# The last eight neighbour pieces of a two-layer graph kernel: three bf16 passes over fp8 masks replaced by one float32r pass over widened masks

## The chip, the cores and the metric

The kernel runs on one core of one Trainium2 chip. The metric is device time of one launch in microseconds (us), the median of three runs. TensorE (PE) multiplies matrices, VectorE (DVE), ScalarE (ACT) and GpSimd (POOL) work on tiles, SyncE (SP) issues the output transfers.

## The reference

There are 4096 nodes with 64 features, and a symmetric adjacency `adj` with ones on the diagonal. Layer 0 is graph attention over 4096 entities, layer 1 sums neighbours:

```python
h = jnp.maximum(_layernorm(x, axis=-1), 0.0)
x = x + gnn0(h, entity_embs, adj, W, a)      # masked softmax over leaky scores, @ entity_embs, + h, elu
h = jnp.maximum(_layernorm(x, axis=-1), 0.0)
x = x + (matmul((adj == 1).astype(x.dtype), h) + h)
```

The change lies in the last line's product, and only in its last eighth by rows of h times all columns.

## The kernel before, in words

Features lie on partitions (64 for one half of a pair of 512 nodes, 64 for the other), nodes along the free axis; there are NP = 4 pairs p of 2 x 512 nodes. The adjacency arrives as 64 chunks of 128 x 2048 fp8 masks and stays in the 27 slots of `am`. The kernel goes through STEPS_ALL = 128 steps: VectorE makes scores (line 938), ScalarE takes their exponential (line 683), TensorE multiplies by the entities (line 1284) and sums denominators (line 1318). Adding own rows to the masks' diagonals is `own` on GpSimd (line 521).

Layer 1 is cut into 32 **pieces** (p, j), in the order written out in `ORDER`: piece v adds the neighbours in block j (512 nodes, four slices of 128) to pair p. Rows of h are kept in `h3` as three bf16 parts (high, middle, low) whose sum is the f32 value. A slice is 12 matmuls (3 parts x 2 halves s x 2 column strips of 32), by `neighbours` (line 1196), with the 128x512 fp8 mask as the moving operand. Pieces 0 to 16 run among the steps. After step 127 come, in TensorE's order: the last denominators (line 1305), slices 0 to 5 of the rest, `spread` (line 1146), slices 6 to 12, `rows_turned` (line 1172), slices 13 to 27, and, once `lasts` on VectorE has written the third part of the last pair's rows (line 909, `h_ready`), slices 28 to 59. The last 32 of them are pieces 24 to 31, two for each pair, because they need blocks j = 6 and 7, which are the last pair's own rows. Piece 19 is the last of pair 0 before the final eight and consists of slices 8 to 11.

Beside them runs the finish of pair 3, which each engine does in its own program order: `sums_out` (ACT, lines 592 to 594), `inverses` (DVE, 860 to 863), `spread` (PE), `weighted` (DVE, 872 and 873), `negatives` (ACT, 606 and 608), `rows_on` (DVE, 878 and 879), `rows_turned` (PE), `rows_normed` (DVE, 888 to 896, with `deviations` on POOL, 512 and 513), then `highs`, `rests`, `middles`, `lasts`. At the end VectorE takes each pair's sums with one instruction (line 990), and SyncE sends it out (line 424):

```python
for p in range(NP):
    dve.wait_ge(piece_done, 26 + 2 * p)
    v.scalar_tensor_tensor(out=yp[:, p, 0:HALF], in0=gather(24 + 2 * p), scalar=-1.0, in1=xs[:, p],
                           op0=ALU.add, op1=ALU.add).then_inc(out_ready, 1)
```

Of the kernel before, what the change touches and what calls it, by code (L numbers as in the profile page):

```python
# [62 lines left out]
def graph_layers(nc, adj_t, xt, ent, w_t, a_cols, eye, out, N, M, D):  # L63
# [110 lines left out]
    with ctx:  # L174
        def sb(name, shape, dt):
            return ctx.enter_context(nc.sbuf_tensor(name, shape, dt))
# [92 lines left out]
        def diagonal(v):  # L269
            p, j = ORDER[v]  # L270
            slot, at = chunk_at(chunk0[j % 2] + j) if p == 0 else chunk_at(chunks_of(p, j)[0])
            step = HALF + P if p == 0 else 2 * HALF + P
            at += slot * UNIT + (j % 2 * HALF if p else 0)
            return am_flat[:, at:at + SUB * step].rearrange("p (i k) -> p i k", k=step)[:, :, 0:P]

        def part(k):
            return h0[:, (0, 1, 0)[k]]
# [131 lines left out]
        def own_at(v):  # L409
            return PIECE_AT[v] - 3  # L410

        block = ctx.enter_context(nc.Block())

        @block.sync
        def _(sp):
            sp.dma_start(enta[:], ent).then_inc(ld_ent, 16)
            sp.dma_start(mats[:], eye).then_inc(ld_eye, 16)
            sp.dma_start(xs[:, 0:1], xt[:, 0:1]).then_inc(ld_x, 16)

            sp.wait_ge(landed[landed_of(chunk0[1] - 1)[0]], landed_of(chunk0[1] - 1)[1])  # L420
            sp.dma_start(xs[:, 1:NP], xt[:, 1:NP]).then_inc(ld_late, 16)
            for p in range(NP):
                sp.wait_ge(out_ready, p + 1)
                sp.dma_start(out[p], yp[:, p, 0:HALF]).then_inc(out_done, 16)
            sp.wait_ge(out_done, 16 * NP)

        @block.gpsimd
        def _(pool):
# [109 lines left out]
                    if w < PIECES and n == own_at(w):  # L538
                        own(w)
            for w in OWN:  # L540
                if PIECES <= w < OPENS[-1] + 2:
                    own(w)
            deviations(NP - 1)
            for w in OWN[6:]:
                own(w)

        @block.scalar
        def _(act):
# [127 lines left out]
            for n in range(STEPS_ALL):  # L676
                b, jt = block_at(n)
                act.wait_ge(y_made, n + 1)
                m = 2 // HALVES[b]
                for r in range(m):  # L680
                    y = yp[:, n % YS, r * HALF:r * HALF + width(b)]
                    at = jt * m + r
                    e = sc.activation(y, y, ACT.Exp, bias=tbias[:, at:at + 1], scale=delta[:, 0:1])  # L683
                e.then_inc(exp_done, 1)
                for p, f in NORM.items():
                    if n == f["sq"]:
                        squares_first(p)
# [24 lines left out]
                if b + 1 < NB:  # L712
                    if b >= 1 and jt == SROWS[b] + 1:
                        s_rows(b)
                    for h in range(first[b + 1], first[b + 2]):
                        if n == VOUT[b + 1]:
                            v_rows(b + 1, h)
            sums_out(NB - 1)
            negatives(NP - 1)
            highs(NP - 1)  # L720
            middles(NP - 1)

        @block.vector
        def _(dve):
# [199 lines left out]
            for n in range(STEPS_ALL):  # L924
# [41 lines left out]
                if b + 1 < NB:  # L966
                    if n == READ[b + 1]:
                        read_sums(b + 1)
                    for h in range(first[b + 1], first[b + 2]):
                        if n == LARGEST[b + 1]:  # L970
                            largest(b + 1, h)
                    if n == LARGEST[b + 1]:
                        shifts(b + 1)
                    if n + 1 == start_of[b + 1]:
                        put_codes(b + 1, 0)
            for r in range(2):
# [3 lines left out]
                v.tensor_tensor(yp[:, SUM_IN[r] % YS], yp[:, n % YS], yp[:, (n + 1) % YS], ALU.add).then_inc(y_summed, 1)  # L980
            inverses(NP - 1)
            weighted(NP - 1)
            rows_on(NP - 1)
            rows_normed()
            rests(NP - 1)
            lasts(NP - 1)
            for p in range(NP):
                dve.wait_ge(piece_done, 26 + 2 * p)

                v.scalar_tensor_tensor(out=yp[:, p, 0:HALF], in0=gather(24 + 2 * p), scalar=-1.0, in1=xs[:, p],  # L990
                                       op0=ALU.add, op1=ALU.add).then_inc(out_ready, 1)

        @block.tensor
        def _(pe):
# [180 lines left out]
            def neighbours(v, i):  # L1175
# [16 lines left out]
                for k in range(3):  # L1192
                    for s in range(2):
                        for d in range(0, D, 32):
                            at = s * D + d
                            mm = t.matmul(gather(v)[at:at + 32, :], h3[:, jt, k * D + d:k * D + d + 32],  # L1196
                                          masks(v, i, s),
                                          start=(v in OPENS and i == 0 and k == 0),
                                          stop=((v in VISITS or j == NH - 1) and i == SUB - 1 and k == 2),
                                          tile_position=(0, at))  # L1200
                if i == SUB - 1:
                    mm.then_inc(piece_done, 1)
# [181 lines left out]
```

## Time and profile before

| | |
|---|---|
| median of 3 runs | 354.31 us (353.14 to 354.66) |
| the profiled execution's own time | 352.26 us |
| its span, first to last instruction | 350.5 us |
| around the span | 1.76 us |
| granted TensorE clock, mean | 1.00 |
| PE / DVE / ACT / POOL busy | 92% / 79% / 58% / 22% of the span |

The profiled execution lies 2.05 us under the median. Times inside the span count from its start. An engine executes its instructions in program order, so a wait holds all that is written behind it on the same engine.

### The profile page before, as it was taken

Reading aid. Unit: us, or ns where it says so; the run is one execution under the profiler, and the core shown is the slowest. Engines: PE = TensorE matmul, PEld = TensorE weight load, DVE = VectorE, ACT = ScalarE, POOL = GpSimd, SP = SyncE. Lnnn points to the kernel's source line nnn. Section 1 sums busy time; section 2 is a strip of 40 time slices with the busy share of each in tenths; the row PEclk is TensorE's granted clock in tenths of the full one; section 3 lists DMA queues with packets and bytes.
Section 4 is the critical chain, followed back from the end, with each engine's and each line's share of the span. In section 5 each row is a group of like instructions: output and inputs, shape, how many; then the busy total and the mean of one; then the engine's idle time right before and its main releaser. Section 6 shows DMA issues by size and latency. Waiting matters only on the chain.

```text
span 350.5 us, 8710 instructions
## 1 busy us (share of the span) xinstructions
PE 322.8 (92%) x3857; PEld 129.0 (37%) x3857; DVE 277.7 (79%) x344; ACT 203.6 (58%) x263; POOL 77.7 (22%) x118
## 2 busy tenths in 40 slices
PE   0279799999999989999999999999999999999996
PEld 0244344333332232342333433443334333345553
DVE  0682799999999999999998799899984999455201
ACT  1010388679959789657865977385749667330000
POOL 4663258821212121013002400000008000004000
PEclk9999999999999999999999999999999999999999
DMA  8999999999999999358003950000000000000011
GB/s 201 113 101 155 127 108 107 108 108 107 108 108 108 107 108 108 37 47 77 2 2 34 90 60 2 2 3 2 2 0 4 0 2 2 2 2 2 2 64 60
DMA packets 10564, 20.85 MB, mean 59 GB/s; under 512 B 1248, under 2 KB 1312, under 8 KB 10400
## 3 DMA queue, kind: packets, MB, share of 16 engines
q0 software_dynamic: 9216, 16.78, 48.4%
q1 hardware_dynamic: 1152, 3.49, 2.8%
q8 instruction: 30, 0.49, 0.6%
q10 hardware_dynamic: 160, 0.03, 0.0%
q14 instruction: 6, 0.05, 0.0%
HBM read 69.58 MB, written 1.05 MB: 202 GB/s over the span
## 4 chain that ended last, share of the span: by engine, by line
PE 50%; DVE 24%; issue 3%; ACT 1%; POOL 1%; DVEq 0%; POOLq 0%
PE pb L1284 18%; DVE yp L938 14%; PE pb L1196 11%; PE pb L1318 8%; PE pa L1196 8%; DVE coded L827 2%; PE pa L1076 1%; PE pa L1161 1%; PE pa L1153 1%; DVE um L806 1%; PE pa L1029 1%; PE pa L1146 1%; DVE rows L851 1%; POOL rstd L513 0%; PE pa L1089 0%
## 5 line engine op out<-in xcount | busy, mean ns | idle before, releaser
L683 ACT ACTIVATE yp<-yp,tbias,delta 128x1024 f32<-128x1024 f32 (+1 forms) x160 | 162.2, 1067 | 36.6 <-DVE yp L938 36.4
L938 DVE SCALAR_TENSOR_TENSOR yp<-s8b,t8neg,coded 128x1024 f32<-128x1024 f32 (+1 forms) x160 | 161.7, 1065 | 1.9 <-PE pb L1318 0.8
L1284 PE MATMUL pb<-yp,enta 128*32 128x512 f32 x1024 | 130.2, 594 | 2.8 <-ACT yp L683 2.6
L1318 PE MATMUL pb<-yp,onesf 128*32 128x512 f32 x496 | 64.6, 593 | 0.0
L1196 PE MATMUL pb<-am,h 128*32 128x512 fp8e4 x960 | 61.1, 379 | 0.0
L449 POOL DMA_DIRECT2D am<-adj_t x64 | 34.7, 556 | 104.8 <-PE pb L1196 53.1
L1284 PEld LDWEIGHTS pb<-yp,enta 128*32 128x32 f32 x1024 | 30.3, 110 | 57.8 <-issue 32.4
L1196 PEld LDWEIGHTS pb<-am,h 128*32 128x32 bf16 x960 | 28.0, 97 | 44.1 <-issue 30.0
L827 DVE TENSOR_TENSOR coded<-am,vx 128x2048 uint16<-128x2048 uint16 (+1 forms) x33 | 41.4, 1255 | 2.4 <-ACT vx L578 1.1
L1196 PE MATMUL pa<-am,h 128*32 128x512 fp8e4 x576 | 33.8, 379 | 0.2 <-DVE h L909 0.2
L512 POOL TENSOR_SCALAR rstd<-rstd 128x8 f32<-128x8 f32 x4 | 2.2, 544 | 126.3 <-ACT rstd L619 78.8
L1318 PEld LDWEIGHTS pb<-yp,onesf 128*32 128x32 f32 x496 | 15.7, 110 | 23.2 <-issue 17.7
L1196 PEld LDWEIGHTS pa<-am,h 128*32 128x32 bf16 x576 | 16.3, 97 | 20.5 <-issue 9.0
L1076 PE MATMUL pa<-am,gtab 128*32 128x512 fp8e4 x256 | 21.2, 411 | 0.9 <-DVE gtab L770 0.9
L1076 PEld LDWEIGHTS pa<-am,gtab 128*32 128x32 bf16 x256 | 6.7, 100 | 17.3 <-issue 15.3
L799 DVE TENSOR_SCALAR gmax<-pa,wk 128x1024 f32<-128x1024 int32 (+1 forms) x5 | 5.3, 1064 | 6.2 <-PE pa L1076 6.2
L513 POOL TENSOR_TENSOR rstd<-rstd,mhalf 128x8 f32<-128x8 f32 x4 | 9.5, 2379 | 0.3
L998 PE MATMUL pa<-num 64*128 64x64 f32 x2 | 0.7, 444 | 9.6 <-DVE num L740 9.6
L521 POOL TENSOR_TENSOR am<-am,eyeb 128x512 fp8e4<-128x512 fp8e4 x8 | 9.5, 1210 | 0.0
L990 DVE SCALAR_TENSOR_TENSOR yp<-pa,xs 128x512 f32<-128x512 f32 x2 | 1.4, 692 | 10.0 <-PE pa L1196 10.0
L606 ACT ACTIVATE tm<-ta 128x512 f32<-128x512 f32 x4 | 2.5, 631 | 11.2 <-DVE ta L873 11.2
L479 POOL TENSOR_TENSOR rstd<-rstd,mhalf 128x8 f32<-128x8 f32 x4 | 8.8, 2193 | 0.3
(184 smaller groups left out, 227.3 us busy)
## 6 DMA issues: line engine op xcount, KB each, us to landing
am<-adj_t POOLq DMA_DIRECT2D x64, 256.0 KB, 22.2
enta<-ent SPq DMA_DIRECT2D x1, 1040.0 KB, 5.1
out<-yp SPq DMA_DIRECT2D x4, 256.0 KB, 2.0
xs<-xt SPq DMA_DIRECT2D x1, 768.0 KB, 9.3
mats<-eye SPq DMA_DIRECT2D x1, 320.0 KB, 7.8
xs<-xt SPq DMA_DIRECT2D x1, 256.0 KB, 11.0
num<-w_t ACTq DMA_DIRECT2D x1, 32.0 KB, 5.3
a_sb<-a_cols ACTq DMA_DIRECT2D x1, 0.5 KB, 8.0
```

Source lines behind the costliest of these rows:

```text
L449: pool.dma_start(am[:, slot, at:at + CHUNK], adj_t[q]).then_inc(landed[landed_of(q)[0]], 16)
L479: g.tensor_tensor(rstd0[:, p], rstd0[:, p], mhalf[:], ALU.pow).then_inc(sd_ready, 1)
L513: g.tensor_tensor(rstd[:], rstd[:], mhalf[:], ALU.pow).then_inc(rstd_ready, 1)
L521: g.tensor_tensor(e, e, eyeb[:].unsqueeze(1).to_broadcast([P, SUB, P]), ALU.add, saturate=False).then_inc(own_ready, 1)
L683: e = sc.activation(y, y, ACT.Exp, bias=tbias[:, at:at + 1], scale=delta[:, 0:1])
L799: link(v.tensor_scalar(gmax[:, 0:W], sums, wk[:], None, ALU.min))
L827: return v.tensor_tensor(coded[:].bitcast(U16).rearrange("p (t i) -> p t i", t=t)[:, lo:hi], am[:, slot_of[U]].bitcast(U16).rearrange("p ( ...
L938: y = v.scalar_tensor_tensor(out=yp[:, n % YS, r * HALF:r * HALF + W], in0=s8b[:, pair(b) % 2, cols(b)], scalar=t8neg[:, at:at + 1], in1=c ...
L1076: mm = t.matmul(pa[g * KC:(g + 1) * KC, first[b] % 2 + i], gtab[:, jt], am[:, slot, at:at + HALF], start=(k == 0), stop=(k == NQ - 1), til ...
L1196: mm = t.matmul(gather(v)[at:at + 32, :], h3[:, jt, k * D + d:k * D + d + 32], masks(v, i, s), start=(v in OPENS and i == 0 and k == 0), s ...
L1284: t.matmul(acc2(b)[k:k + 32, :], enta[:, at, d:d + 32], yp[:, n % YS, s * HALF:(s + 1) * HALF], start=(jt == 0), stop=final, tile_position ...
L1318: mm = t.matmul(dens[at:at + 32, :], onesf[:, 0:32], yp[:, (m + r) % YS, s * HALF:(s + 1) * HALF], start=(opens and m + batch == n + 1), s ...
```

## The change

The last eight pieces (v = 24 to 31, slices counted k = 0 to 31) no longer go through `neighbours`. The last pair's rows are stored in `hr` as two float32r parts side by side, high in columns 0 to 63 and rest in columns 64 to 127, and one matmul of 128 rows x 128 columns x 512 gives both products for one half: 2 matmuls a slice, 64 in all, each with its mask as a float32r tile. The masks are widened from fp8 by copies of 128 x 1024 elements (two of 128 x 512 for pair 0). They go into 12 free slots of `am` and the 7 buffers `yp`, so 19 (ROOM) fit; slice k from 19 on takes the place of slice k - 19 and waits for `slice_done`. Each pair's two halves sit in two PSUM banks, in which the two parts still have to be added, and pair 2 reuses pair 0's banks.

Three steps of the old finish (`highs`, `rests`/`middles`/`lasts` of the last pair) become one ScalarE copy and one VectorE subtraction (`hr_ready`). GpSimd's last `own` calls for pieces 30 and 31 come ahead of `deviations`.

```diff
+        FREE = sorted((k for k in range(SLOTS) if k not in late_slots), key=slot_done)
+        ROOM = len(FREE) + YS
+        def wide_masks(k):
+            r = k % ROOM
+            return amr[:, FREE[r]] if r < len(FREE) else ypr[:, r - len(FREE)]
+        EARLY = dict(d0=(0,), a0=(1, 3, 5, 7, 9), p0=(2, 6, 10), d1=(4, 8, 11), a1=(12, 13), d2=(14,),
+                     a2=(15, 16, 17, 18))
+        LATE = range(ROOM, 32)
+        LATE_BY = {k: "adap"[(k - ROOM) % 4] for k in LATE}
+        def last_bank(p, s):
+            return (pb[:, 2 * s], pa[:, 2 + s])[p % 2]
+        def wait_wide(eng, k):
+            v, i = slice_of(k)
+            if k >= ROOM:
+                eng.wait_ge(slice_done, k - ROOM + 1)
+            elif k < len(FREE):
+                eng.wait_ge(piece_done, slot_done(FREE[k]) + 1)
+                eng.wait_ge(coded_ready, NU)
+            else:
+                eng.wait_ge(pv_done, STEPS_ALL)
+            if v in OWN:
+                eng.wait_ge(own_ready, OWN.index(v) + 1)
 ...gpsimd, behind the loop over the steps
             for w in OWN:
-                if PIECES <= w < OPENS[-1] + 2:
+                if w >= PIECES:
                     own(w)
+            for k in EARLY["p0"]:
+                widen(k)
             deviations(NP - 1)
-            for w in OWN[6:]:
-                own(w)
+            for k in late("p"):
+                widen(k)
 ...scalar
+            for k in EARLY["a0"]:
+                widen(k)
             sums_out(NB - 1)
+            for k in EARLY["a1"]:
+                widen(k)
             negatives(NP - 1)
-            highs(NP - 1)
-            middles(NP - 1)
+            for k in EARLY["a2"]:
+                widen(k)
+            act.wait_ge(hh_ready, NP)
+            sc.copy(hr[:, :, 0:D], natural(NP - 1)[0]).then_inc(high_ready, 1)
+            for k in late("a"):
+                widen(k)
 ...vector, in rows_normed, ahead of the wait for rstd_ready
+                sums_so_far(3)
+                sums_so_far(1)
 ...vector, behind the steps
+            def sums_so_far(p):
+                last = max(w for w in range(LAST) if ORDER[w][0] == p)
+                dve.wait_ge(piece_done, last + 1)
+                v.scalar_tensor_tensor(out=xs[:, p], in0=gather(last), scalar=-1.0, in1=xs[:, p],
+                                       op0=ALU.add, op1=ALU.add).then_inc(so_far, 1)
+            def last_sums(p):
+                for s in range(2):
+                    if p == NP - 1 and s == 0:
+                        dve.wait_ge(half_done, 1)
+                    else:
+                        dve.wait_ge(slice_done, 8 * (p + 1))
+                    own, other = slice(s * D, (s + 1) * D), slice((1 - s) * D, (2 - s) * D)
+                    link(v.tensor_tensor(xs[own, p], last_bank(p, s)[other], xs[own, p], ALU.add))
+                    o = v.tensor_tensor(s8b[own, p // 2, ...], last_bank(p, s)[own], xs[own, p], ALU.add)
+                    if s:
+                        o.then_inc(out_ready, 1)
+            widen 0
             (the two sums of line 980)
+            widen 4, 8, 11
             inverses(NP - 1)
+            widen 14
             weighted(NP - 1)
+            sums_so_far(0)
             rows_on(NP - 1)
             rows_normed()
-            rests(NP - 1)
-            lasts(NP - 1)
-            (one instruction of line 990 for each pair)
+            dve.wait_ge(high_ready, 1)
+            v.tensor_tensor(hr[:, :, D:2 * D], natural(NP - 1)[0], hr[:, :, 0:D].bitcast(F32),
+                            ALU.subtract).then_inc(hr_ready, 1)
+            sums_so_far(2)
+            widen 20, 24
+            last_sums(0)
+            widen 28
+            last_sums(1), last_sums(2), last_sums(3)
 ...tensor
-            pieces(range(13, (len(ORDER) - PIECES) * SUB))
+            pieces(range(13, (LAST - PIECES) * SUB))
+            pe.wait_ge(hr_ready, 1)
+            for p in range(NP):
+                if p >= 2:
+                    pe.wait_ge(out_ready, p - 1)
+                both_halves = [(k, s) for k in range(8 * p, 8 * p + 8) for s in range(2)]
+                if p == NP - 1:
+                    both_halves.sort(key=lambda ks: ks[1])
+                for k, s in both_halves:
+                    pe.wait_ge(wide[e], BY[e].index(k) + 1)
+                    mm = t.matmul(last_bank(p, s), hr[:, k % 8], wide_masks(k)[:, s * HALF:(s + 1) * HALF],
+                                  start=(k % 8 == 0), stop=(k % 8 == 7))
```

## Rows read from the trace of the kernel before

**Rows 1.** The page's busy tenths in 40 slices of the span.

```profile
PE   0279799999999989999999999999999999999996
DVE  0682799999999999999998799899984999455201
PEclk9999999999999999999999999999999999999999
```

**Rows 2.** The chain that ended last: start, length in us, what.

```profile
301.94 3.43 PE pb L1284 x32
...
306.24 3.89 PE pa L1196 x72
...
311.11 4.65 PE pa L1196 x84
...
326.41 10.54 PE pa L1196 x192
347.36 0.69 DVE yp L990
```

**Rows 3.** Busy time by engine in the last stretch of TensorE.

```profile
326.40:347.40 21.00, 20.90 (x384) 11.44 (x384) 2.11 (x4) 0.00 (x0) 0.00 (x0) 1.00 0.11 40
```

**Rows 4.** Timeline from the last masks' coding to the third part of h.

```profile
292.52 1.23 DVE L827 TENSOR_TENSOR coded<-am,vx 128x2048 uint16<-128x2048 uint16 x1
...
298.79 1.28 DVE L938 SCALAR_TENSOR_TENSOR yp<-s8b,t8neg,coded 128x1024 f32<-128x1024 f32 x1 [0.85 <-PE pb L1318]
300.11 1.25 ACT L683 ACTIVATE yp<-yp,tbias,delta 128x1024 f32<-128x1024 f32 x1 [0.89 <-DVE yp L938]
...
306.30 0.58 ACT L592 COPY rows<-pb 64x512 f32<-64x512 f32 x1 [4.95 <-PE pb L1305]
...
310.05 0.15 PEld L1146 LDWEIGHTS pa<-rows,mats 64*32 64x32 f32 x8 [0.42 <-DVE rows L863]
...
313.95 0.69 DVE L878 SCALAR_TENSOR_TENSOR ta<-ta,tm 128x512 f32<-128x512 f32 x1 [1.36 <-ACT tm L608]
314.68 0.69 DVE L879 TENSOR_TENSOR xs<-ta,xs 128x512 f32<-128x512 f32 x1
...
315.69 0.66 PE L1172 MATMUL pa<-mats,xs 128*128 128x128 f32 x4
...
316.28 4.72 PE L1196 MATMUL pa<-am,h 128*32 128x512 fp8e4 x84
...
321.74 2.60 POOL L521 TENSOR_TENSOR am<-am,eyeb 128x512 fp8e4<-128x512 fp8e4 x2
321.86 1.52 DVE L896 TENSOR_TENSOR rs<-tm,rstd 128x512 f32<-128x512 f32 x1 [1.88 <-POOL rstd L513]
...
324.06 0.82 DVE L904 TENSOR_TENSOR rs<-rs,h 128x512 f32<-128x512 f32 x1 [0.68 <-ACT h L636]
```

**Rows 5.** Timeline of 128-column f32 weights: loads and matmuls.

```profile
35.64 1.62 PEld L1207 LDWEIGHTS pb<-enta,onesf 128*128 128x128 f32 x8
35.75 1.92 PE L1207 MATMUL pb<-enta,onesf 128*128 128x260 f32 x8
```

**Rows 6.** Groups of instructions by form: busy, mean ns.

```profile
L683 ACT ACTIVATE yp<-yp,tbias,delta 128x1024 f32<-128x1024 f32 x96 | 115.5, 1240 | 28.7 <-DVE yp L938 28.5
...
L636 ACT CAST h<-rs 128x512 bf16<-128x512 f32 x4 | 2.5, 618 | 9.6 <-DVE rs L896 9.5
...
L851 DVE TENSOR_SCALAR rows<-vx 3x1024 bf16<-3x1024 uint8 x3 | 2.0, 674 | 0.0
```

**Rows 7.** Timeline where GpSimd and VectorE work at once, two places.

```profile
47.46 5.37 DVE L938 SCALAR_TENSOR_TENSOR yp<-s8b,t8neg,coded 128x512 f32<-128x512 f32 x8
50.58 2.32 POOL L478 TENSOR_SCALAR rstd<-rstd 128x8 f32<-128x8 f32 x1 [1.86 <-ACT rstd L657]
...
158.88 3.29 DVE L827 TENSOR_TENSOR coded<-am,vx 128x2048 uint16<-128x2048 uint16 x1
158.90 2.18 POOL L521 TENSOR_TENSOR am<-am,eyeb 128x512 fp8e4<-128x512 fp8e4 x2
```

More of the change, by code:

```diff
@@ L8 @@
 BF16 = mybir.dt.bfloat16
+F32R = mybir.dt.float32r
 FP8 = mybir.dt.float8e4
@@ L182, in sem @@
             return ctx.enter_context(nc.semaphore(name))
-        am = sb("am", [P, SLOTS, UNIT], FP8)
-        coded = sb("coded", [P, UNIT], U8)
-        yp = sb("yp", [P, YS, 2 * HALF], F32)
+        with ExitStack() as loop_only:
+            am = loop_only.enter_context(nc.sbuf_tensor("am", [P, SLOTS, UNIT], FP8))
+            coded = loop_only.enter_context(nc.sbuf_tensor("coded", [P, UNIT], U8))
+            yp = loop_only.enter_context(nc.sbuf_tensor("yp", [P, YS, 2 * HALF], F32))
+        amr = sb("amr", [P, SLOTS, 2 * HALF], F32R)
+        hr = sb("hr", [P, 2 * SUB, 2 * D], F32R)
+        ypr = sb("ypr", [P, YS, 2 * HALF], F32R)
         s8b = sb("s8b", [P, 2, 2 * HALF], F32)
@@ L274, in diagonal, with slot_done, slice_of, narrow_masks @@
             return am_flat[:, at:at + SUB * step].rearrange("p (i k) -> p i k", k=step)[:, :, 0:P]
+        LAST = 24
+        late_slots = {chunk_at(q)[0] for v in range(PIECES, len(ORDER)) for q in chunks_of(*ORDER[v])}
+        def slot_done(k):
+            return max(last_piece(U) for U in range(NU) if slot_of[U] == k)
+        FREE = sorted((k for k in range(SLOTS) if k not in late_slots), key=slot_done)
+        ROOM = len(FREE) + YS
+        def slice_of(k):
+            return LAST + 2 * (k // 8) + k % 8 // SUB, k % SUB
+        def wide_masks(k):
+            r = k % ROOM
+            return amr[:, FREE[r]] if r < len(FREE) else ypr[:, r - len(FREE)]
+        def narrow_masks(k):
+            v, i = slice_of(k)
+            w = wide_masks(k)
+            if ORDER[v][0] == 0:
+                return [(w[:, s * HALF:(s + 1) * HALF], masks(v, i, s)) for s in range(2)]
+            slot, at = chunk_at(chunks_of(*ORDER[v])[i // 2])
+            at += i % 2 * 2 * HALF
+            return [(w, am[:, slot, at:at + 2 * HALF])]
+        EARLY = dict(d0=(0,), a0=(1, 3, 5, 7, 9), p0=(2, 6, 10), d1=(4, 8, 11), a1=(12, 13), d2=(14,),
+                     a2=(15, 16, 17, 18))
+        LATE = range(ROOM, 32)
+        LATE_BY = {k: "adap"[(k - ROOM) % 4] for k in LATE}
+        def late(e):
+            return [k for k in LATE if LATE_BY[k] == e]
+        BY = {e: [k for n in sorted(EARLY) if n[0] == e
+                  for k in EARLY[n]] + late(e) for e in "adp"}
+        def last_bank(p, s):
+            return (pb[:, 2 * s], pa[:, 2 + s])[p % 2]
         def part(k):
@@ L395, in graph_layers @@
         out_ready = sem("out_ready")
+        wide = {e: sem(f"wide_{e}") for e in "adp"}
+        slice_done = sem("slice_done")
+        half_done = sem("half_done")
+        so_far = sem("so_far")
+        high_ready = sem("high_ready")
+        hr_ready = sem("hr_ready")
         def unit_of(j):
@@ L410, in own_at @@
             return PIECE_AT[v] - 3
+        def wait_wide(eng, k):
+            v, i = slice_of(k)
+            if k >= ROOM:
[7 more added lines that the diff above has]
+                eng.wait_ge(own_ready, OWN.index(v) + 1)
         block = ctx.enter_context(nc.Block())
@@ L423, in _ @@
                 sp.wait_ge(out_ready, p + 1)
-                sp.dma_start(out[p], yp[:, p, 0:HALF]).then_inc(out_done, 16)
+                sp.dma_start(out[p], s8b[:, p // 2, p % 2 * HALF:(p % 2 + 1) * HALF]).then_inc(out_done, 16)
             sp.wait_ge(out_done, 16 * NP)
@@ L540, in _, with widen @@
             for w in OWN:
-                if PIECES <= w < OPENS[-1] + 2:
+                if w >= PIECES:
                     own(w)
+            def widen(k):
+                wait_wide(pool, k)
+                for dst, src in narrow_masks(k):
+                    w = g.tensor_copy(dst, src)
+                w.then_inc(wide["p"], 1)
+            for k in EARLY["p0"]:
+                widen(k)
             deviations(NP - 1)
-            for w in OWN[6:]:
-                own(w)
+            for k in late("p"):
+                widen(k)
         @block.scalar
@@ L717, in _, with widen @@
                             v_rows(b + 1, h)
+            def widen(k):
+                wait_wide(act, k)
+                for dst, src in narrow_masks(k):
+                    w = sc.copy(dst, src)
+                w.then_inc(wide["a"], 1)
+            for k in EARLY["a0"]:
+                widen(k)
             sums_out(NB - 1)
+            for k in EARLY["a1"]:
+                widen(k)
             negatives(NP - 1)
-            highs(NP - 1)
-            middles(NP - 1)
+            for k in EARLY["a2"]:
[4 more added lines that the diff above has]
+                widen(k)
         @block.vector
@@ L975, in _, with widen @@
                         put_codes(b + 1, 0)
+            def widen(k):
+                wait_wide(dve, k)
+                for dst, src in narrow_masks(k):
+                    w = v.tensor_copy(dst, src)
+                w.then_inc(wide["d"], 1)
+            def sums_so_far(p):
+                last = max(w for w in range(LAST) if ORDER[w][0] == p)
+                dve.wait_ge(piece_done, last + 1)
+                if p == NP - 1:
+                    dve.wait_ge(hn_ps, NP)
+                v.scalar_tensor_tensor(out=xs[:, p], in0=gather(last), scalar=-1.0, in1=xs[:, p],
[8 more added lines that the diff above has]
+                    link(v.tensor_tensor(xs[own, p], last_bank(p, s)[other], xs[own, p], ALU.add))
+                    o = v.tensor_tensor(s8b[own, p // 2, p % 2 * HALF:(p % 2 + 1) * HALF], last_bank(p, s)[own],
+                                        xs[own, p], ALU.add)
+                    if s:
+                        o.then_inc(out_ready, 1)
+            for k in EARLY["d0"]:
+                widen(k)
             for r in range(2):
@@ L980, in _ @@
                 v.tensor_tensor(yp[:, SUM_IN[r] % YS], yp[:, n % YS], yp[:, (n + 1) % YS], ALU.add).then_inc(y_summed, 1)
+            for k in EARLY["d1"]:
+                widen(k)
             inverses(NP - 1)
+            for k in EARLY["d2"]:
+                widen(k)
             weighted(NP - 1)
+            sums_so_far(0)
             rows_on(NP - 1)
             rows_normed()
-            rests(NP - 1)
-            lasts(NP - 1)
[L987 to L991, printed above, removed]
+            dve.wait_ge(high_ready, 1)
+            v.tensor_tensor(hr[:, :, D:2 * D], natural(NP - 1)[0], hr[:, :, 0:D].bitcast(F32),
+                            ALU.subtract).then_inc(hr_ready, 1)
+            sums_so_far(2)
+            dve.wait_ge(so_far, NP)
+            d = late("d")
+            for k in d[0:2]:
+                widen(k)
+            last_sums(0)
+            for k in d[2:]:
+                widen(k)
+            for p in range(1, NP):
+                last_sums(p)
         @block.tensor
@@ L1198, in neighbours @@
                                           start=(v in OPENS and i == 0 and k == 0),
-                                          stop=((v in VISITS or j == NH - 1) and i == SUB - 1 and k == 2),
+                                          stop=((v in VISITS or j == NH - 3) and i == SUB - 1 and k == 2),
                                           tile_position=(0, at))
```

6 lines of the change are left out of this document (added).

## The prediction

> **What bounds the kernel now.** I read the page's busy tenths first, then the chain that ended last, then the busy time of the last stretch, then the timeline from 292 us on. The page shows TensorE at nine tenths in nearly every slice from 125 us to the end, at full granted clock, and VectorE falling away in the last sixth [rows 1]. The chain says the same of the end: from 301.9 us it consists of TensorE's matmuls but for a passage through VectorE, and after the last matmul only one instruction of VectorE and the output transfer follow [rows 2]. The last eight pieces are 384 matmuls in 20.90 us with no idle time, and the other compute engines have 2.11 us of work between them there [rows 3]. So TensorE bounds the stretch that is changed, and nothing else is near it.
>
> The stretch ahead of it (306 to 326 us) is TensorE's too, but barely. `spread` loads its weights at 310.05, released by the inverse, and in the chain slices 0 to 5 run until 310.13 (306.24 + 3.89). `rows_on` ends at 315.37 (314.68 + 0.69), the transposes start at 315.69, which is when slices 6 to 12 run out (311.11 + 4.65). Two meeting points, with slack of 0.1 and 0.3 us [rows 2, 4]. Whatever makes the finish of pair 3 later there is paid in full.
>
> **TensorE's last stretch.** Removed: 32 slices of 12 matmuls. 72 of them take 3.89 us, so a slice takes 0.648 us, and four strips of 512 columns side by side take 0.216 us, one column per cycle of 2.4 GHz [rows 2]. Added: 64 float32r matmuls with 512 columns each. No row has one. Its price is bounded from below by the one-pass products' 0.216 us, and from above by one record of an f32 product: an f32 product is two records here, four strips take 3.43 us / 32 x 4 = 0.429 us a record, so a whole f32 product costs 0.858 us, four times a one-pass one [rows 2]. If f32 is four partial products, float32r, given here two parts cut by hand, is one of them: I take 0.216. A second price is the weight load: each matmul loads 128 x 128 f32 weights. The eight records of 260 columns with such weights take 1.92 us, 0.24 us or less each, and their loads lie beside them [rows 5]. A load thus fits behind 0.22 us of matmul, and I charge nothing; exposed it would be charged to each of the 64. So a slice takes 0.43 us instead of 0.648, and the 32 take 13.8 us.
>
> The rows give 0.216 by an argument and not by a measurement. The Trainium skill, FP8 and Floating Point Precision, section TensorE Precision Notes, says that true FP32 is four passes and that reduced-precision FP32 reads 4 bytes and truncates to FP22; the trace agrees with the four. By it the stretch is the same 13.8 us.
>
> **Its tail is VectorE's.** The old end is one 0.69 us instruction for a pair. The new one is four for a pair (`last_sums`), each on 64 partitions x 512 with a PSUM input; at 0.69 us (line 878, same columns) plus 0.03 between them, 0.72 [rows 4]. Let T be the start of the float32r matmuls. Pair 0 ends at T + 3.46, its sums at T + 6.6, before pair 2 wants the banks (T + 6.9). Widening 28 (0.67) and pair 1's sums run to T + 10.2, before pair 3's matmuls at T + 10.37. Pairs 2 and 3 then give eight instructions in a row from T + 10.37 + 0.23 (release as before: 326.41 + 384 x 0.054 = 347.13, then 347.36 [rows 2, 3]): end at T + 10.6 + 8 x 0.72 = T + 16.36. TensorE itself is done at T + 13.8. So VectorE becomes the end's bound: 2.56 us lie behind TensorE's end instead of 0.92, and 1.6 of the 7.1 us that TensorE saves are lost.
>
> **Widening.** ScalarE: a cast of 512 takes 0.618, a 1024 instruction 1.24 with a bias [rows 6]; I take 0.61 and 1.04 (0.618 + 512 x 0.83 ns; bounds 0.9 and 1.24). VectorE: one source in SBUF, 1024 elements, 0.674, and 0.41 for half of it [rows 6]; the upper bound is 1.28, the two-source price [rows 4]. GpSimd: no row of this size; from ScalarE's 0.61 to 1.09 for 512 (half of 2.18, two sources) [rows 6, 7]; I take 0.8, 1.6 for 1024. Late ones: ScalarE has seven, each freed by slice k - 19; 31 is freed at T + 5.6 and wanted at T + 13. At 1.04 each it is done by T + 9. VectorE has three, GpSimd three (freed at T + 1.7, 3.4, 5.2, wanted 7.7 us later). TensorE waits for none. GpSimd's 22 may overlap VectorE's 24; I charge 0.25 for that.
>
> **What the early ones do to the finish.** This is where the change costs.
> 1. ScalarE does slices 1, 3, 5, 7, 9 ahead of `sums_out`. Its last exponential ends at 301.36, `sums_out` starts at 306.30: 4.94 us of room [rows 4]. The work is 8 x 0.61 + 1.04 = 5.9 us, with starts overlapping a little or gaps of 0.03: `sums_out` starts 0.75 to 1.25 late, I take 1.0. The inverse is late by it, and so is `spread`, which has no slack: TensorE stands for 1.0 us.
> 2. GpSimd now does own 31 (released at 293.75, when the last masks are coded) and slices 2, 6, 10 there, 1.1 + 4 x 0.8 + 1.6 = 5.9 us beside VectorE's last steps [rows 4]. The two get in each other's way: a coding instruction (1.23 elsewhere [rows 4]) took 3.29 beside GpSimd's 2.18, so it waited for nearly all of it; elsewhere a 0.2 us job of GpSimd took 2.32 and VectorE's eight ran at 0.67 as always [rows 7]. Who loses differs. VectorE had 0.85 us to spare before its last step [rows 4]. If it loses 3.5 us (four instructions each behind one of GpSimd), the last exponential is 2.6 late; if it wins, nothing. I take 0.6, added to point 1, since ScalarE has no room left.
> 3. `sums_so_far(0)` stands ahead of `rows_on` and waits for piece 19, that is for slice 11, six slices after `spread`. Without shifts slice 11 ends at 311.11 + 3.89 = 315.0, VectorE starts at 315.2; then 0.72, 0.72, 0.69: 317.33 instead of 315.37. TensorE wants it at 315.69 and gets it at 317.4: stands for 1.7 us. It is relative to `spread`, so it adds to points 1 and 2.
>
> At no cost: slice 0 on VectorE (the last step ends at 300.07 or 0.6 later, then 0.82 and the two sums of line 980, 1.28 at most each: 304.1, while TensorE wants them at 301.94 + 3.43 = 305.4 [rows 2, 4]); 4, 8, 11 (2.2 us from there to 306.3, and the denominators are copied out by 306.30 + 2 x 0.6 = 307.5, 1.6 later with the shifts); 14 (in the wait for `spread`); 12, 13 on ScalarE (2.1 us; `sums_out` ends after three copies at 308.1, `negatives` are two instructions of 0.65 that end at 313.92: 4.5 us between them [rows 4]); 15 to 18 (4.2 us, while VectorE norms for 8 us, 315.37 to 323.38); `sums_so_far(3)` and `(1)` in the wait for the reciprocal root (1.9 us [rows 4]), though (1) waits for slice 19 and ends about when the root does. The rows: cast 0.62, subtraction 0.83 [rows 4, 6] end 9.5 us after `rows_on`, and 0.7 earlier without own 30 and 31 beside line 896. TensorE comes 10.7 us after `rows_on` (transposes 0.6, 15 slices 9.7, 0.3), so the two dropped steps win nothing: there the end was TensorE's slices already.
>
> **Sum.** T without shifts is 316.28 + 15 x 0.648 = 326.0. With 1.0 + 0.6 + 1.7 it is 329.3. The end of VectorE's last instruction is 329.3 + 16.36 + 0.25 = 345.9, against 348.05: 2.15 us less. The profiled execution goes from 352.26 to 350.1, and 2.05 us lie between it and the median: 354.31 - 2.15 = 352.2. A measurement of this kernel can tell 0.5% (1.8 us) from no change, so faster is under 352.5 and slower over 356.1; the forecast is just over the line.
>
> A page speaks against the change. The Trainium skill, Advanced Engine Details and Errata, section VectorE Performance Modes (Mode Summary), notes that VectorE's second SBUF port is GpSimd's too and that GpSimd and two-port instructions of VectorE block each other. The case above in which coding took 3.29 us agrees, with two sources as well. What it would do here is rival B.
>
> **Rivals.**
> A. The front costs little: ScalarE's copies fit the 4.94 us and only point 3 stays (T = 327.7), or that goes too. End 344.3 to 342.6, so 350.6 to 348.9. For it: starts may overlap; against: 5.9 us of work in 4.9. Chance 0.13.
> B. GpSimd's 5.9 us come on top of VectorE's last steps: point 2 is 2.6 instead of 0.6, 354.2. If all of it does (5.9 - 0.85 = 5.1), 356.7. Chance 0.17.
> C. The other side: the float32r matmul isn't 0.216. T + 64c + 0.23 + 1.44 (half 0 of pair 3 is summed meanwhile) equals the old 348.05 at c = 0.267 us; above it the kernel is slower. At 0.429, two cycles per column as in an f32 record, the end is 329.3 + 27.5 + 1.7 = 358.5: 364.7. If the load stays exposed (1.62 us / 8 = 0.2 at most, 0.11 if half overlaps), c is 0.33 to 0.42, 358.3 to 364. For it: no row shows four-byte columns faster than two cycles. Chance 0.11.
> D. Late widening or the banks hold TensorE: 1 to 2 us, 353.7. Chance 0.07.
> The forecast, 350.7 to 353.7, has 0.52. Of it, 0.35 are under 352.5. With A: faster 0.48. B's first half, D and the rest: same 0.39. C and the end of B: slower 0.13. The range, 349.3 to 356.0, leaves out C and the ends of A and B.
>
> **What would show it.** PE L1196 loses 384 matmuls and 64 of 128x512 f32 come in their place, 0.216 us apart; at 0.43 C holds. ScalarE's copy of line 592 starts about 1.6 us later than 306.30 and directly behind a widening; if behind a wait for TensorE, A holds. VectorE waits for TensorE ahead of `sums_so_far(0)`, and TensorE stands about 1.7 us ahead of the transposes. VectorE's last eight instructions are back to back. VectorE instructions of lines 938 and 980 over 1.3 us beside GpSimd's copies speak for B. Wrong at once: a lower granted clock after the two stands of TensorE; before it there is none [rows 1].

## The result, and the profile after

The median went from 353.48 us (8 runs, 352.15 to 355.18) to 351.15 us (8 runs, 350.55 to 352.32): a ratio of 0.9938, with a 95% interval of 0.9916 to 0.9961, 2.2 us less by the ratio (1.4 to 3.0). The forecast was 0.994. The profiled execution took 351.37 us, with a span of 349.6. The part that is changed is larger than the text ahead of the prediction says: pieces 24 to 31 are 8 of 32 and take blocks 6 and 7 of 8, so it is the last quarter of the product by rows of h, not the last eighth.

The page of the changed kernel, busy tenths in 40 slices of 8.74 us:

```profile
PE   0379799999999989999999999999999999988994
DVE  0781897999999999999998789899985999976586
ACT  1010477688959689666865978285839585875160
PEclk9999989999999999999999999999999999999999
```

VectorE, which was down to 0 to 2 tenths at the end [rows 1], now has 5 to 8. TensorE has an 8 at slices 36 and 37, where it stood. The chain that ended last, from the last masks' coding on (start, length, what; parts under 0.1 us left out where marked):

```profile
295.82 3.60 DVE yp L1031 x3
...
300.88 1.64 DVE yp L1031
...
303.69 5.19 ACT amr L798 x9
...
308.90 0.58 ACT rows L668
...
312.63 1.06 PE pa L1281 x8
313.70 4.03 PE pa L1331 x72
317.73 0.02 issue
317.75 0.69 DVE xs L1082
...
319.82 0.66 PE pa L1307 x4
320.48 4.65 PE pa L1331 x84
325.12 5.18 PE pb L1331 x96
330.30 3.86 PE pb L1480 x16
334.16 3.63 PE pa L1480 x16
337.79 3.64 PE pb L1480 x16
341.43 0.02 issue
341.45 0.70 DVE xs L1092
...
346.46 0.69 DVE s8b L1093
```

This is the new course of the end. VectorE's steps lead to ScalarE's nine copies (line 798), those to `sums_out` (668) and, through the inverse, to `spread` (1281); six slices (72 matmuls) lead to `sums_so_far(0)` (1082) and only that to the transposes (1307). From 330.3 it is the float32r matmuls (1480), and after pair 2's it leaves TensorE and goes through eight instructions of VectorE to the end; the last 16 matmuls aren't on it.

The runs differ early, so I count from an anchor: the start of the last 32 f32 matmuls of the steps, 301.76 in the old trace, 302.36 in the new one. Times behind it, in us:

| | before | after |
|---|---|---|
| last denominators (L1305 / L1440) | 3.43 | 4.40 |
| `sums_out` (L592 / L668) | 4.54 | 6.54 |
| `spread` (L1146 / L1281) | 8.29 | 10.27 |
| transposes (L1172 / L1307) | 13.93 | 17.46 |
| first matmul of the last eight pieces (L1196 / L1480) | 24.65 | 27.88 |
| end of VectorE's last instruction | 46.29 | 44.79 |

From the anchor on the changed kernel is 1.50 us shorter; 0.60 of that does not show between the two profiled executions, because the second reached its anchor later.

The timeline of the changed kernel shows the three places where TensorE stood (0.78 us ahead of the last denominators, 0.92 ahead of `spread`, 1.48 ahead of the transposes):

```profile
288.24 5.72 DVE L1031 SCALAR_TENSOR_TENSOR yp<-s8b,t8neg,coded 128x1024 f32<-128x1024 f32 x4
288.35 2.14 POOL L588 TENSOR_TENSOR am<-am,eyeb 128x512 fp8e4<-128x512 fp8e4 x1 [15.49 <-DVE coded L918]
...
295.36 1.42 POOL L588 TENSOR_TENSOR am<-am,eyeb 128x512 fp8e4<-128x512 fp8e4 x1 [4.88 <-DVE coded L918]
...
295.74 6.77 DVE L1031 SCALAR_TENSOR_TENSOR yp<-s8b,t8neg,coded 128x1024 f32<-128x1024 f32 x4
...
296.73 7.43 POOL L614 CAST amr<-am 128x512 fp32r<-128x512 fp8e4 x5
...
302.55 1.24 ACT L759 ACTIVATE yp<-yp,tbias,delta 128x1024 f32<-128x1024 f32 x1 [0.31 <-DVE yp L1031]
...
306.76 1.06 PE L1440 MATMUL pb<-yp,onesf 128*32 128x512 f32 x8 [0.78 <-DVE yp L1104]
...
308.90 0.58 ACT L668 COPY rows<-pb 64x512 f32<-64x512 f32 x1
...
317.75 0.69 DVE L1082 SCALAR_TENSOR_TENSOR xs<-pa,xs 128x512 f32<-128x512 f32 x1 [2.57 <-PE pa L1331]
...
319.82 0.66 PE L1307 MATMUL pa<-mats,xs 128*128 128x128 f32 x4 [1.48 <-DVE xs L970]
```

Four of VectorE's step instructions took 6.77 us beside GpSimd's copies, where one took 1.28 [rows 4], and the last exponential ended 1.43 us behind the anchor instead of 0.40 ahead of it (301.36). `sums_out` has no wait in brackets: it follows ScalarE's own copies. VectorE waited 2.57 us for slice 11, and TensorE 1.48 us for VectorE.

In the old kernel there was one stand in this stretch too, which the rows ahead of the prediction leave out. Slices 13 to 27 ran out at 326.0 us, `lasts` ended at 326.26, and TensorE began the last eight pieces at 326.41, released by it:

```profile
325.57 0.69 DVE L909 TENSOR_TENSOR h<-rs,h 128x512 bf16<-128x512 f32 x1 [0.69 <-ACT h L641]
...
326.41 10.54 PE L1196 MATMUL pa<-am,h 128*32 128x512 fp8e4 x192 [0.24 <-DVE h L909]
```

The float32r matmuls by line (duration, first and last start), 26 of the 64:

```profile
L1480 PEld LDWEIGHTS pb<-amr,hr x26: 186/188/189, 330.2 to 340.8; 128*128 128x128 f32 x26
L1480 PE MATMUL pb<-amr,hr x26: 389/389/501, 330.2 to 341.0; 128*128 128x512 f32 x26
```

The 64 run from 330.24 to 345.04; less one duration of 0.39 that is 14.41 / 63 = 0.229 us apart, not 0.429 and not quite 0.216. The mean holds one longer gap of 0.34 us behind the first; the median gap is 0.227, the figure in the expectations below.

### The profile page after: what moved, and what is told of

The parts are those of the page before. It is cut to its first block, busy times and chain, and to the rows that moved or that the text cites. A ratio compares the mean times of both kernels' runs of the same rounds, so it can differ in the third digit from the quotient of the medians.

```text
span 349.6 us, 8138 instructions
## 1 busy us (share of the span) xinstructions
PE 319.3 (91%) x3537; PEld 130.6 (37%) x3537; DVE 296.4 (85%) x369; ACT 220.8 (63%) x284; POOL 91.3 (26%) x126
## 4 chain that ended last, share of the span: by engine, by line
PE 36%; DVE 33%; ACT 5%; issue 4%; DVEq 0%; ACTq 0%
DVE yp L1031 21%; PE pb L1419 12%; PE pb L1331 9%; PE pb L1453 6%; DVE coded L918 3%; PE pa L1331 2%; PE pb L1480 2%; ACT yp L759 2%; ACT amr L798 1%; PE pa L1480 1%; PE pa L1288 1%; PE pa L1211 1%; DVE xs L1092 1%; DVE s8b L1093 1%; DVE um L897 1%
## 5 line engine op out<-in xcount | busy, mean ns | idle before, releaser
L1031 DVE SCALAR_TENSOR_TENSOR yp<-s8b,t8neg,coded 128x1024 f32<-128x1024 f32 (+1 forms) x160 | 164.4, 1082 | 1.1
L1331 PE MATMUL pb<-am,h 128*32 128x512 fp8e4 x768 | 50.6, 379 | 0.0
L1331 PEld LDWEIGHTS pb<-am,h 128*32 128x32 bf16 x768 | 22.2, 97 | 39.5 <-issue 29.9
L579 POOL TENSOR_SCALAR rstd<-rstd 128x8 f32<-128x8 f32 x4 | 1.1, 274 | 99.6 <-ACT rstd L695 79.9
L1331 PE MATMUL pa<-am,h 128*32 128x512 fp8e4 x384 | 23.3, 379 | 0.0
L1331 PEld LDWEIGHTS pa<-am,h 128*32 128x32 bf16 x384 | 10.6, 97 | 15.4 <-issue 8.3
L798 ACT CAST amr<-am 128x512 fp32r<-128x512 fp8e4 (+1 forms) x15 | 11.0, 814 | 3.7 <-PE pb L1480 3.7
L546 POOL TENSOR_TENSOR rstd<-rstd,mhalf 128x8 f32<-128x8 f32 x4 | 12.7, 3170 | 0.3
L614 POOL CAST amr<-am 128x512 fp32r<-128x512 fp8e4 (+1 forms) x8 | 10.6, 1345 | 8.1 <-PE pb L1480 7.3
L580 POOL TENSOR_TENSOR rstd<-rstd,mhalf 128x8 f32<-128x8 f32 x4 | 9.4, 2362 | 0.3
L654 ACT CAST vx<-pa 128x512 uint8<-128x512 f32 x8 | 4.3, 574 | 7.0 <-PE pa L1242 7.0
```

The lines of the kernel that those rows point to most:

```text
L546: g.tensor_tensor(rstd0[:, p], rstd0[:, p], mhalf[:], ALU.pow).then_inc(sd_ready, 1)
L614: w = g.tensor_copy(dst, src)
L798: w = sc.copy(dst, src)
L1031: y = v.scalar_tensor_tensor(out=yp[:, n % YS, r * HALF:r * HALF + W], in0=s8b[:, pair(b) % 2, cols(b)], scalar=t8neg[:, at:at + 1], in1=c ...
```

## The experiments

All are edits of the changed kernel. Where no number of runs is given, the time is of one run. The times alone scatter by over 1 us, so what is compared first is the time behind the anchor, in us:

| | sums_out | spread | transposes | first of the last eight pieces | end |
|---|---|---|---|---|---|
| before | 4.54 | 8.29 | 13.93 | 24.65 | 46.29 |
| after | 6.54 | 10.27 | 17.46 | 27.88 | 44.79 |
| e1 | 6.52 | 10.25 | 15.89 | 26.31 | 43.22 |
| e2 | 4.71 | 8.44 | 15.63 | 26.04 | 42.96 |
| e3 | 5.52 | 9.27 | 16.46 | 26.87 | 43.79 |
| e4 | 4.54 | 8.29 | 13.93 | 24.34 | 41.27 |
| c1 | 5.20 | 8.93 | 16.12 | 26.53 | 43.44 |
| g1 | 5.51 | 9.24 | 16.43 | 26.84 | 43.75 |
| n1 | 6.54 | 10.27 | 17.46 | 27.87 | 44.13 |
| n2 | 6.54 | 10.27 | 17.46 | 27.87 | 44.86 |
| n3 | 4.54 | 8.29 | 13.93 | 24.35 | 40.61 |
| e5 | 4.54 | 8.29 | 13.93 | 24.34 | 40.59 |
| n4 | 4.54 | 8.29 | 13.93 | 24.35 | 39.78 |

**e1**, `sums_so_far(0)` behind `rows_on`:

```diff
-            sums_so_far(0)
             rows_on(NP - 1)
+            sums_so_far(0)
```

> sums_so_far(0) moved behind rows_on, where VectorE waits for the transposes anyway. Ledger theory (each stand of TensorE ahead of its meeting point is a cost of its own): in the changed kernel the transposes start 7.19 us after spread (312.63 to 319.82), here 5.6 us, so the float32r matmuls start 1.55 us earlier relative to spread, and the end is 1.5 us earlier. Rival (the chain of rows was as late anyway, a loss moves to the next meeting point): the transposes are earlier, but TensorE then stands ahead of the float32r matmuls, and the end is less than 0.5 us earlier.

Measured: 348.64 us. From `spread` to the transposes 5.64 us instead of 7.19, and the end 1.57 us earlier, both counted behind the anchor: the whole stand comes back. The ledger theory holds. The instruction itself costs nothing there:

```profile
316.04 0.69 DVE L970 TENSOR_TENSOR xs<-ta,xs 128x512 f32<-128x512 f32 x1
316.65 0.68 DVE L1082 SCALAR_TENSOR_TENSOR xs<-pa,xs 128x512 f32<-128x512 f32 x1
317.05 0.42 PEld L1307 LDWEIGHTS pa<-mats,xs 128*128 128x128 f32 x4 [0.42 <-DVE xs L970]
```

**e2**, GpSimd idle early:

```diff
-  p0=(2, 6, 10), ... a2=(15, 16, 17, 18)
+  p0=(), ... a2=(15, 16, 17, 18, 2, 6, 10)
-                if w >= PIECES:
+                if PIECES <= w < LAST:
                     own(w)
             deviations(NP - 1)
+            (own(w) for w >= LAST)
```

> GpSimd makes no early copies (slices 2, 6, 10 go to ScalarE behind 15 to 18) and adds the own rows of pieces 30 and 31 behind the reciprocal root, as before the change. Ledger theory (GpSimd beside VectorE's last steps made those late): the last steps of line 1031's kind take 1.28 us each again instead of up to 2, the last exponential ends about 2 us earlier, TensorE's stand of 0.8 us ahead of the last denominators goes, and the stand ahead of spread becomes under 1 us instead of 0.93 behind the 0.78: end 1.5 to 2.0 us earlier. Rival (ScalarE's five copies alone make sums_out late): less than 0.5 us.

Measured: 350.45 us, and 1.83 us less behind the anchor. The steps are what they were before:

```profile
295.75 3.67 DVE L1034 SCALAR_TENSOR_TENSOR yp<-s8b,t8neg,coded 128x1024 f32<-128x1024 f32 x3
...
301.58 1.25 ACT L762 ACTIVATE yp<-yp,tbias,delta 128x1024 f32<-128x1024 f32 x1 [0.89 <-DVE yp L1034]
...
302.73 5.19 ACT L801 CAST amr<-am 128x512 fp32r<-128x512 fp8e4 x9
...
307.94 0.58 ACT L671 COPY rows<-pb 64x512 f32<-64x512 f32 x1
```

ScalarE's five slices are still ahead of `sums_out`, take 5.19 us, and make it 0.17 late (4.71 against 4.54). So they alone cost 0.17, and GpSimd's work on top of them 1.83.

**e3**, ScalarE's copies spread out: `a0=(1, 3), a1=(5, 7, 9), a2=(12, 13, 15, 16, 17, 18)`.

> ScalarE makes only slices 1 and 3 ahead of sums_out, 5, 7, 9 behind it, 12 and 13 behind negatives. Ledger theory: sums_out waits for TensorE and no longer for ScalarE; spread starts 0.9 to 1.2 us earlier relative to the last denominators, the 0.8 us stand ahead of those stays, end 1.0 us earlier. Rival (VectorE's copies 4, 8, 11 end just then and hold the inverse): the inverse waits for VectorE instead, under 0.4 us.

Measured: 349.83 us, 1.00 us less behind the anchor; `sums_out` now has a wait for TensorE in its bracket:

```profile
307.32 0.58 ACT L668 COPY rows<-pb 64x512 f32<-64x512 f32 x1 [2.04 <-PE pb L1440]
```

As expected. Its 1.0 and e2's 1.83 are not two costs: GpSimd's work makes ScalarE start late, and ScalarE's copies pass the lateness on. Either cure takes away the part that goes through ScalarE; the rest of the 2.00 (0.98 in e3) is the late last denominators.

**e4**, the three together.

> The three together. Ledger theory: all stands between 302 and 330 us go (0.8 + 0.9 + 1.5, and the slack), the float32r matmuls start where slices 13 to 27 would end without any, near 326.2 us plus what the run is late before, the tail stays 16.9 us: 3.5 to 4 us under the changed kernel, about 347.4 us where it is 351.2, 6 us under the old one. Rival (gains don't add, the rows of h become the bound of the float32r start): 2 us under the changed kernel at most.

Measured: 349.51 us (6 runs, 347.06 to 350.25), ratio to the old kernel 0.9874 (0.9837 to 0.9911). `sums_out`, `spread` and the transposes are the old kernel's to 0.01 us. The float32r matmuls start 3.54 us earlier than in the changed kernel, when slices 13 to 27 are done, and 0.31 us earlier than the old kernel's last eight pieces. 3.52 us less behind the anchor, as the ledger has it; the rival falls. The medians show less than that (1.6 us), because e4's runs had the lower granted clock of the last section more often. At the same mean clock the difference is there: at 0.998 to 0.999 the changed kernel took 350.55 to 350.94 us and e4 347.06, at 0.994 they took 352.22 to 352.32 and 348.61 to 349.21.

**c1**, own rows of 30 and 31 late, GpSimd's copies early, and **g1**, the reverse (p0 empty, own rows early as in the change).

> The changed kernel, but GpSimd adds the own rows of pieces 30 and 31 behind the reciprocal root again; its five copies stay where they are. It tells which of GpSimd's jobs make VectorE's last steps late: two of 512 elements with two sources (3.6 us busy), or five copies (7.4 us busy). Theory (copies): sums_out starts within 0.6 us of the changed kernel's 6.54 us behind the anchor (the start of the last 32 f32 matmuls of the steps). Rival (own rows): it starts at 5 us or below.

> GpSimd adds the own rows of pieces 30 and 31 early as in the changed kernel, but makes no early copies (they go to ScalarE behind 15 to 18). With own rows late and copies early sums_out started 5.2 us behind the anchor, with neither 4.71, with both 6.54. Theory (the two jobs use up one and the same slack of VectorE, so each alone costs little and only both together cost 1.8 us): here 4.7 to 5.2. Rival (the two-source additions are the dear ones): 5.9 to 6.1.

Measured: 349.27 and 349.42 us. `sums_out` is at 5.20 with the copies alone and 5.51 with the own rows alone, 4.71 with neither, 6.54 with both: 0.49, 0.80 and 1.83. Both statements of c1 were off (copies are not the dear part, own rows are not all of it), and g1 lies between its two. Together the jobs cost more than the sum of both (1.29). The durations of VectorE's steps show why:

```profile
L1034 DVE SCALAR_TENSOR_TENSOR yp<-s8b,t8neg,coded x9: 1279/1285/1630, 284.9 to 298.8; 128x1024 f32<-128x1024 f32 x9
L1031 DVE SCALAR_TENSOR_TENSOR yp<-s8b,t8neg,coded x9: 1271/1275/2129, 284.8 to 299.3; 128x1024 f32<-128x1024 f32 x9
```

In c1 (first line) four steps took 1.63 us beside the copies, in g1 (second line) two took 2.13 beside the additions, and all others 1.28. So VectorE lost 4 x 0.35 = 1.4 us in c1, 2 x 0.85 = 1.7 in g1, and 2 x 0.85 + 3 x 0.35 = 2.75 in the changed kernel, which had both. Its slack of 0.85 us [rows 4] is there only once: 0.55, 0.85 and 1.9 are left, and the last exponential ended 0.48, 0.78 and 1.82 us later than in e2.

**n1**, pair 2's fold left out:

```diff
+                    if p != 2:
                         link(v.tensor_tensor(xs[own, p], last_bank(p, s)[other], xs[own, p], ALU.add))
```

> Leaves out the two adds of the second part to pair 2's sums (2 of VectorE's last 8 instructions, so pair 2's output lacks that part). Theory (VectorE sets the end, TensorE is 0.7 us behind it): from the first float32r matmul to the end 16.3 us instead of 16.9, after which pair 3's second half waits for TensorE. Rival (TensorE or the output sets it): 16.9 us.

Measured: 350.03 us; first matmul to end 16.26 instead of 16.91. Two instructions of 0.69 less gave 0.65, since then VectorE waits for TensorE:

```profile
343.20 0.68 DVE L1094 TENSOR_TENSOR s8b<-pa,xs 64x512 f32<-64x512 f32 x1
343.86 0.39 PE L1481 MATMUL pa<-ypr,hr 128*128 128x512 f32 x1
344.29 0.68 DVE L1093 TENSOR_TENSOR xs<-pa,xs 64x512 f32<-64x512 f32 x1 [0.40 <-PE pa L1481]
```

**n2**, `hr[:, k % 8, 0:D]` as weights, written to the first 64 partitions of each bank; the other 64 are not written, so the output is not the product.

> The float32r matmuls take the high part alone as weights (64 columns instead of 128; the rest part is left out of the result). It tells why they come 0.227 us apart and not 0.216. Theory (the load of 128 columns of four bytes, 0.188 us beside each matmul, costs the difference): 0.216 apart, TensorE's last matmul 0.6 to 0.7 us earlier behind the first. Rival (four-byte columns cost it themselves): 0.227 again.

Measured: 353.6 us; TensorE is busy for 14.94 us instead of 14.80. The load fell from 188 to 134 ns and the pace did not get better (median gap 0.230 us, not 0.227): my theory of the load falls. The rival's 0.227 was not met exactly either.

**n3**, two bf16 parts, masks as they are:

```diff
-                    mm = t.matmul(last_bank(p, s), hr[:, k % 8], wide_masks(k)[:, s * HALF:(s + 1) * HALF],
+                    mm = t.matmul(last_bank(p, s), hr[:, k % 8, 0:2 * D], masks(v, i, s),
```

> No float32r and no widening: the rows in two bf16 parts (high and middle; the low part is left out) side by side as weights of 128 columns, the masks in fp8 as they are, sums_so_far(0) behind rows_on, GpSimd's own rows of 30 and 31 late. It shows what is left of the plan without any widening, and the pace of a two-byte 128-column pass. Theory: the meeting points are those of the old kernel (3.4, 8.3, 13.9 us behind the anchor), 0.216 us a matmul, 16.4 us from the first of them to the end, 40.8 us from anchor to end. Rival (the pace of 0.227 belongs to 128-column weights of any type): 41.3.

Measured: 348.54 us. 13.99 us from the first of the 64 matmuls to TensorE's end, (13.99 - 0.38) / 63 = 0.216 apart with the same 128 columns of weights. So 0.013 us a matmul, 0.8 us in 64, belongs to the float32r operands and not to the width of the weights. And the meeting points are e4's: in e4 widening costs nothing beside that pace. It also shows where TensorE's gain comes from: the old slice of 0.648 us is three times 0.216, one for each bf16 part, and two parts take two, in bf16 as in float32r.

**e5**, e4 with ScalarE's help for pair 2, and **n4**, n3 with the same:

```diff
+            act.wait_ge(slice_done, 24)
+            for s in range(2):
+                f = sc.copy(num[own], last_bank(2, s)[other])
+            f.then_inc(folded, 1)
 ...vector, for pair 2
+                for s in range(2):
+                    o = v.tensor_tensor(xs[own, 2], last_bank(2, s)[own], xs[own, 2], ALU.add)
+                link(o)
+                dve.wait_ge(folded, 1)
+                v.tensor_tensor(s8b[:, 1, 0:HALF], num[:], xs[:, 2], ALU.add).then_inc(out_ready, 1)
```

> e4 and ScalarE copies pair 2's two other halves out of PSUM side by side, so VectorE needs three instructions for pair 2 instead of four. Theory (VectorE's eight instructions in a row set the end, 0.65 us to be had before TensorE does): from the first float32r matmul to the end 16.25 us instead of 16.93, anchor to end 40.6, the time 0.6 us under e4 and 13 us per thousand under the old kernel. Rival (ScalarE's copies come too late, or the two read PSUM in each other's way): 16.9 or more.

> n3 (two bf16 parts side by side, the low part left out, no widening, no stands) with the same help of ScalarE. Theory: 15.6 us from the first matmul of the last eight pieces to the end, anchor to end 39.9 us, 6.4 us under the old kernel and 0.7 under e5. Rival: the pace or the tail is not what sets it, 40.6.

Measured: e5 346.43 us (5 runs, 346.07 to 348.02), ratio 0.9795 (0.9772 to 0.9818); n4 345.54 us (5 runs), ratio 0.9776 (0.9752 to 0.9799). In e5 16.25 us from first matmul to end, in n4 15.43. e5 in the trace:

```profile
336.80 1.39 DVE L1098 TENSOR_TENSOR xs<-pb,xs 64x512 f32<-64x512 f32 x2 [0.79 <-PE pb L1499]
336.80 1.18 ACT L820 COPY num<-pb 64x512 f32<-64x512 f32 x2 [3.72 <-PE pb L1499]
338.22 0.69 DVE L1101 TENSOR_TENSOR s8b<-num,xs 128x512 f32<-128x512 f32 x1
```

Both engines read the same banks from 336.80 on, and neither is slower for it (0.69 and 0.58 us an instruction, as elsewhere). e5 computes what the changed kernel does and beats both kernels: its interval lies under the changed kernel's 0.9916 to 0.9961. n4 is 0.81 us shorter still behind the anchor, though the two intervals overlap; it carries two bf16 parts of each row instead of two float32r parts.

## Why the prediction was right

- **The pace of TensorE.** Taken as 0.216 between 0.216 and 0.429; measured 0.229. The argument (one of four partial products) held, rival C is out. TensorE's stretch became 6.1 us shorter (20.91 to 14.80), not 7.1. The 6% over it costs 48 x 0.013 = 0.6 us up to the end of pair 2. The Trainium skill, FP8 and Floating Point Precision, section TensorE Precision Notes, pointed the same way; the trace agrees with one pass in place of four, 0.229 against 0.858 us.
- **The weight load behind the matmul**: right, 0.188 us beside each, and n2 shows that it doesn't set the pace.
- **VectorE sets the end**: right. Eight instructions back to back from 341.45, 0.72 us apart; n1 and e5 show 0.65 us before TensorE does. Predicted 16.36 + 0.25 from the first matmul, measured 16.91: the pace cost more, and the 0.25 for a late slice 24 didn't come (pair 3's matmuls follow pair 2's without a gap).
- **Late widening holds nobody**: right. 1024 elements took 1.04 us on ScalarE, 0.70 on VectorE and, where the estimate had no row, 1.04 on GpSimd instead of 1.6.
- **Point 1, ScalarE's early copies, 1.0 us**: wrong in size. Alone they cost 0.17 (e2). The work was priced one copy after the other; nine of them took 5.19 us, not 5.9, as each starts before the last has ended: 0.52 apart for 0.61 of duration. That spreading them out gave 1.00 (e3) is no proof of the 1.0: there they pass on GpSimd's delay.
- **Point 2, GpSimd beside VectorE, 0.6 us**: wrong in size, 1.83. This was rival B's mechanism, at 1.83 of its 2.6. The prediction had 5.9 us of GpSimd's work beside the steps. It was 11.0: own 30 came there too, the two additions took 2.14 and 1.42 us, and the copies 7.43, with 1.60 us for each of 512 elements, taken as 0.8. So VectorE and GpSimd both lost. Points 1 and 2 together: 1.6 predicted, 2.00 measured.
- **Point 3, `sums_so_far(0)`, 1.7 us**: 1.55, and e1 gives it back whole.
- **The dropped steps of h win nothing**: wrong, by 0.3 us. The prediction took the third part of h to be there before TensorE came. In the old trace it came 0.26 us after the slices had run out (326.26 against 326.0). The "passage through VectorE" in its first paragraph is this chain, 10 us long, and it held the last eight pieces. In e4 `hr` is ready at 327.44, TensorE comes at 328.65, 0.31 us earlier behind the anchor than before. The sum of the prediction had the gain all the same, since it took T from the slices (326.0) and not from the 326.41 of the trace. In the changed kernel `hr` was ready at 328.0 (327.31 + 0.69), and TensorE came at 330.24.

The sum of the stands was 3.3 and came to 27.88 - 24.34 = 3.54; the tail was 0.3 longer; without stands the start is 24.34 and not 24.24. So the forecast of 2.15 us less meets 1.50 in the one pair of traces and 2.2 (1.4 to 3.0) over the runs. Of the terms that failed, points 1 and 2 nearly cancelled (0.8 too much, 1.2 too little), and that the median fell so near the forecast is partly luck.

The warning of the Trainium skill, Advanced Engine Details and Errata, VectorE Performance Modes, was the one to weigh more. The Trainium skill, GPSIMD Engine Reference, section Specifications, puts it nearer to this case: contention with VectorE instructions that have two SBUF inputs. The trace agrees: with two such inputs (scores and codes) line 1031 went from 1.28 to a median of 1.62 and at most 2.13 us beside GpSimd:

```profile
L1031 DVE SCALAR_TENSOR_TENSOR yp<-s8b,t8neg,coded x9: 1272/1624/2128, 285.7 to 300.9; 128x1024 f32<-128x1024 f32 x9
```

## What to carry to other kernels

TensorE's last matmul would have come 6.4 us earlier without any stand (45.56 behind the anchor before, 39.16 in e4), 6.1 of it by the faster product and 0.3 by the shorter finish of h. The end moved by a quarter of that (1.5), because the work that feeds it was put ahead of meeting points with slack of 0.1 to 0.3 us (3.5): find the instruction that the bound engine waits for next, put nothing ahead of it on its engine, and, where VectorE reads two inputs as here, nothing on GpSimd beside it. A helper instruction with a wait of its own belongs behind the one that others wait for, even if its data are ready about then. And if a product leaves parts to be added outside of PSUM, price those adds behind the last matmul: here they took back the other 1.4 us.

## What the runs showed that I had not expected

The scatter goes with the granted clock. In all traces with a mean of 0.999 or 1.00 the anchor comes at 301.2 to 301.8 us; where the mean is 0.990 to 0.995 it comes at 302.4 to 304.5. While TensorE works, the lower clock is in one place, 44 to 52 us. Here are first the changed kernel, then the old one, in stretches of 4 us, then e4 in stretches of 10 us (busy time of the engines, then the clock; 1.00 is 2.4 GHz, 0.50 is 1.2):

```profile
40.00:44.00 4.00, 2.45 (x22) 0.95 (x18) 4.00 (x7) 3.23 (x6) 1.05 (x2) 1.00 1.06 108
44.00:48.00 4.00, 4.00 (x26) 1.66 (x30) 3.97 (x7) 3.69 (x8) 2.75 (x2) 0.57 1.06 107
```

```profile
40.00:44.00 4.00, 2.45 (x26) 0.59 (x18) 4.00 (x7) 2.74 (x6) 0.92 (x2) 1.00 1.06 109
44.00:48.00 4.00, 4.00 (x44) 1.89 (x40) 3.97 (x6) 4.00 (x8) 2.12 (x3) 1.00 1.06 107
```

```profile
40.00:50.00 10.00, 8.45 (x58) 3.25 (x50) 9.97 (x15) 8.09 (x15) 4.64 (x4) 0.73 1.06 107
50.00:60.00 10.00, 10.00 (x106) 4.78 (x95) 6.72 (x10) 5.91 (x10) 8.44 (x12) 0.92 1.06 109
```

In the 4 us ahead of the fall TensorE stood once for 1.55 us, waiting for an exponential (4.00 less 2.45). In the profiled execution of the old kernel it stood for the same 1.55 us, and the clock stayed at 1.00, so what decides is not shown. The lower clock comes in some runs of every kernel that ran more than once, and no edit here touches that stretch. Why e4's runs had it more often than the changed kernel's stays open. Of e4's six runs, the one with a mean of 0.999 took 347.06 us, the two with 0.994 took 348.61 and 349.21, the three with 0.990 took 349.81 to 350.25. So a comparison of two profiled executions by their spans can be 2 us off, and the anchor is needed. The stands of TensorE that the change brought (0.78, 0.92 and 1.48 us) did not lower the clock: it was 1.00 from there until after the last matmul.

What makes float32r 0.229 us for 512 columns instead of 0.216 stays open: not the load of the weights (n2) nor their width (n2, n3); the type of the weights and that of the moving masks were not tried apart.
